# A two-layer gated attention and mixture kernel: results of the first mixture scattered to (choice, token) order, masks counted in the attention, values kept on chip

## The reference, cut to what matters

```python
x = x + tanh(g_xattn[0]) * attn0(layernorm(x), ctx, ctx)          # causal: query i sees keys 0..i
x = x + tanh(g_ffn[0])   * moe0(layernorm(x))                     # 8 experts, 2 choices, silu(a)*b, F = 1024
x = x + tanh(g_xattn[1]) * attn1(layernorm(x), ctx, ctx, mask)    # mask 2048x1601 int32, 0 = not seen
x = x + tanh(g_ffn[1])   * moe1(layernorm(x))                     # 16 experts, 2 choices, capacity 320, shared MLP

# moe0
topk_vals, topk_idx = top_k(xf @ wr.T, 2);  gates = softmax(topk_vals)
for e in range(8):
    a, b = split(xf @ w1[e] + b1[e]);  y_e = (silu(a) * b) @ w2[e] + b2[e]
    out += sum(where(topk_idx == e, gates, 0)) * y_e
```

## Time and profile before

| | us |
|---|---|
| median of 3 runs | 1788.0 (1787.66 to 1790.7) |
| profiled execution, its own time | 1806.31 |
| its span (first to last instruction) | 1804.6 |
| PE busy in the span | 1481.2 |
| DVE busy | 865.0 |
| ACT busy | 669.3 |
| GpSimd busy | 369.1 |
| mean granted TensorE clock | 0.90 of full |

### The profile page before, as it was taken

How to read it: one execution, slowest core, us unless ns; L and a number is a source line. 1 busy time by engine, 2 the same in 40 slices (tenths; PEclk the granted TensorE clock), 3 DMA queues, 4 the chain that set the end, 5 groups by cost and what they waited for, 6 DMA issues and landing times. The chain is left out here.

```text
span 1804.6 us, 25617 instructions
## 1 busy us (share of the span) xinstructions
PE 1481.2 (82%) x8697; PEld 902.9 (50%) x8698; DVE 865.0 (48%) x2072; ACT 669.3 (37%) x1100; POOL 369.1 (20%) x335
## 2 busy tenths in 40 slices
PE   4588999999996454999999994049999766999994
PEld 2343333333335333999999994022333353566662
DVE  4489998888715321222222224439887455211112
ACT  3224556667762011233222221033778421022221
POOL 0000000000020344057705003400000233425531
PEclk9879999999998566999999997577999886999997
DMA  3811203020032349045503201331110031124434
GB/s 108 255 51 43 93 12 112 1 90 3 1 106 95 108 161 233 24 147 195 206 23 111 96 23 44 109 107 35 37 37 2 11 108 39 54 82 140 137 96 155
DMA packets 92052, 157.50 MB, mean 87 GB/s; under 512 B 12102, under 2 KB 71040, under 8 KB 89791
## 3 DMA queue, kind: packets, MB, share of 16 engines
q1 hardware_dynamic: 68959, 77.19, 14.1%
q0 software_dynamic: 19296, 70.86, 11.5%
q10 hardware_dynamic: 3712, 8.39, 1.2%
HBM read 109.29 MB, written 50.12 MB: 88 GB/s over the span
## 5 line engine op out<-in xcount | busy, mean ns | idle before, releaser
L800 DVE TENSOR_REDUCE mxp<-psA 128x1 f32<-128x384 f32 (+4 forms) x640 | 334.7, 577 | 61.2 <-PE psA L656 41.8
L774 ACT ACTIVATE Pt<-psC 128x1024 f32<-128x1024 f32 (+4 forms) x296 | 256.2, 918 | 146.1 <-PE psC L689 74.9
L1353 PE MATMUL psA<-xTt,w 128*128 128x128 f32 x1728 | 203.3, 278 | 4.7 <-issue 4.4
L1353 PEld LDWEIGHTS psA<-xTt,w 128*128 128x128 f32 x1728 | 198.5, 194 | 11.1 <-issue 11.1
L656 PE MATMUL psA<-Kst,Qst 97*128 97x384 bf16 (+4 forms) x640 | 181.6, 350 | 27.1 <-DMA Qst<-q_parts 12.7
L800 DVE TENSOR_REDUCE mxpt<-psA 128x1 f32<-128x449 f32 x256 | 145.2, 619 | 33.9 <-PE psA L656 28.9
L682 PE MATMUL psC<-Qst,Kst 100*128 100x512 bf16 (+4 forms) x592 | 148.9, 355 | 0.7 <-ACT Pt L774 0.2
L1429 DVE SCALAR_TENSOR_TENSOR hT<-psA,b,sil 128x128 f32<-128x128 f32 x216 | 64.2, 345 | 166.3 <-ACT sil L1407 166.3
L774 ACT ACTIVATE Ptt<-psC 128x1024 f32<-128x1024 f32 (+1 forms) x128 | 123.8, 1020 | 47.5 <-PE psC L682 47.1
L656 PEld LDWEIGHTS psA<-Kst,Qst 97*128 97x128 bf16 x640 | 55.3, 99 | 171.2 <-DVE mxp L800 122.6
L705 PE MATMUL psO<-Pt,Vaug 128*17 128x512 f32 (+4 forms) x1184 | 140.8, 546 | 0.0
(11 more groups left out here) (281 smaller groups left out, 2062.8 us busy)
## 6 DMA issues: line engine op xcount, KB each, us to landing
w<-L_w POOLq DMA_DIRECT2D x8, 2048.0 KB
mi<-mask POOLq DMA_DIRECT2D x16, 800.5 KB, 4.9
Kst<-k_parts SPq DMA_DIRECT2D x12, 800.5 KB, 19.1
w<-L_w POOLq DMA_DIRECT2D x8, 1024.0 KB
q_parts<-parts ACTq DMA_DIRECT2D x4, 1536.0 KB, 14.9
Qst<-q_parts SPq DMA_DIRECT2D x48, 128.0 KB, 2.7
Qstt<-q_parts SPq DMA_DIRECT2D x48, 128.0 KB, 2.8
wg<-L_w_gate POOLq DMA_DIRECT2D x16, 352.0 KB
```

Of the source, the lines that this page charges most:

```text
L774: act.activation(Pt[0:kw, n % SLOTS, :, col:QC], psC[0:kw, n % 2, :].rearrange("p (y t) -> p y t", y=2)[:, :, col:QC], ACT.Exp).then_inc(p ...
L800: dve.tensor_reduce(mxp[:, q, h, pc:pc + 1], psA[:, place_of[("piece", n)] % AB, 0:w], AX.X, ALU.max).then_inc(a_free, 1)
L1353: mmi = pe.matmul(bank(j)[:, i * P:(i + 1) * P], w1[:, side, k, f * P:(f + 1) * P], xTt[:, z, k, :], start=(k == 0), stop=(k == KD - 1))
```

## The change

- `Vaug` is one buffer for the whole kernel. The block "c" computes the keys first and the values last, and leaves the values in `Vaug`; their store to DRAM and their reload are gone. Its key parts lie in the room of `Kst`. The block no longer waits until the key parts have landed in DRAM: SP waits for that at the start of `experts0`, then fills the constant rows of `Kst` from a small DRAM copy, and loads the six key parts in three portions behind the weights of experts 3, 4 and 5.
- The weights of the first mixture are loaded by SP, those of experts 0 and 1 in the block of `route`.
- The rows of the first mixture carry labels; GpSimd's scatter runs in four groups of eight, each with an IOTA and a copy ahead of it. In the loop of `experts0` ACT loads rows and labels, DVE multiplies by the gate in a second instruction, and GpSimd scatters the results to `ys` in (choice, token) order. `combine` reads whole chunks on SP and ACT and adds them.
- Mask counting and the bias addition move to GpSimd's program in the attention (the bias in both attentions, the mask in the first).
- The unneeded rows of `ys0` are no longer zeroed.

```diff
+        Vaug = sb(ctx, "Vaug", [P, NKT, H, NV])
-        def load_key_stack(queue, l, Ks, done):
-            for b, (_, kp) in enumerate(PAIRS):
+        def load_key_stack(queue, l, Ks, done, at=0, most=len(PAIRS)):
+            for b in range(at, at + most):
+                kp = PAIRS[b][1]
...
# projections(): the block called "c" keeps its parts in the room of Kst
+                if ql is None:
+                    room = Kst[:, :, :].rearrange("p h s -> p (h s)")
+                    n_parts = NB * 3 * S
+                    parts = room[:, 0:n_parts].rearrange("p (b t s) -> p b t s", b=NB, t=3)
...
+                def stored(eng):
+                    for b in range(NB):
+                        eng.wait_ge(sto[b], 16 * (len(jobs) // NB))
                     @block.sync
...
-                        if ql == 1:
-                            sp.dma_start(Vaug[:, 0:S // P, :, :].rearrange("p j h n -> p j (h n)"),
-                                         Vs[0:S // P].rearrange("j p n -> p j n")).then_inc(vload, 16)
...
+                            sp.dma_start(k_rows_d[0:1, :], zero_row[:, :]).then_inc(rload, 16)
+                            sp.dma_start(k_rows_d[1:4, :], ones_row[:, :]).then_inc(rload, 16)
-                        if kl == 1:
-                            for j, (k0, kw) in enumerate(key_tiles()):
-                                sp.wait_ge(vev, j + 1)
-                                sp.dma_start(Vs[j, 0:kw, :], vout[0:kw, j % VB, :, :].rearrange("p h n -> p (h n)"))\
-                                  .then_inc(v_sto[j % VB], 16)
...
-                        for b in range(NB):
-                            sp.wait_ge(sto[b], 16 * (len(jobs) // NB))
+                        if ql is not None:
+                            stored(sp)
...
                     def _(pe):
-                        if kl == 1:
-                            pe.wait_ge(ld, 48)
-                            values()
...
-                        if kl == 0:
+                        if kl is not None:
                             values()
                     def _(dve):
-                        if kl == 1:
-                            values()
                         for i in range(len(jobs)):
                             split(i)
-                        if kl == 0:
+                        if kl is not None:
                             values()
# attention(): its gpsimd program
                 pool.memset(ones_q[:, :], 1.0).then_inc(ones_made, 1)
+                pool.wait_ge(ones_made, 1)
+                beside(pool)
# output_projection()
-                        sp.dma_start(bob[:, :], w["bo"].rearrange("(a n) -> a n", a=1).to_broadcast([P, D]))\
-                          .then_inc(ld, 16)
-                    @block.gpsimd
...
-                            if c == 1:
-                                dve.wait_ge(bias_s, 1 + NC)
# new, called as beside() in the first attention
+        def count_masks(st):
...
+                pool.memset(ignored[:, :], 0.0).then_inc(counted, 1)
+                pool.wait_ge(counted, 1)
+                load_mask(0)
+                load_mask(1)
+                for t in range(NQT):
+                    pool.wait_ge(mask_ld[t % 2], 16 * (t // 2 + 1))
+                    pool.tensor_scalar(off[:, :], mi[:, t % 2, :], 0, None, ALU.is_equal).then_inc(seen, 1)
+                    pool.wait_ge(seen, t + 1)
+                    pool.tensor_tensor(ignored[:, :], ignored[:, :], off[:, :], ALU.add).then_inc(counted, 1)
+                    pool.wait_ge(counted, t + 2)
+                    if t + 2 < NQT:
+                        load_mask(t + 2)
# attention_layer()
+                def add_bias(pool):
+                    pool.dma_start(bob[:, :], W[L]["bo"].rearrange("(a n) -> a n", a=1).to_broadcast([P, D])).then_inc(bias_ld, 16)
+                    pool.wait_ge(bias_ld, 16)
+                    pool.tensor_scalar(bob[:, :], bob[:, :], gates[:, L:L + 1], 0.0, ALU.mult, ALU.add).then_inc(bias_s, 1)
...
+                        def beside(pool):
+                            add_bias(pool)
+                            count(pool)
# route(): the first mixture's scatter now takes the labelled form too
-                    if width == D:
-                        for t in range(NQT):
-                            for k in range(2):
-                                scatter_tile(pool, t, k)
-                        return
# experts0(), gpsimd program
+                        with pool.Fori(0, pair_count(pool)) as it:
+                            for z in range(2):
+                                pool.wait_ge(ye, it * 2 + (z + 3))
+                                pool.sem_inc(leaving, 1)
+                                pool.indirect_dma_start(
+                                    ys[:, :], bass.IndirectOffsetOnAxis(ap=lab[:, z, 0:1].bitcast(U32), axis=0),
+                                    yv[:, z, :], None, bounds_check=2 * T - 1, oob_is_err=False).then_inc(y_st[z], 16)
+                            for z in range(2):
+                                pool.wait_ge(y_st[z], it * 16 + 16)
+                                pool.sem_inc(yv_free[z], 1)
# experts0(), sync program
-                        for z in range(2):
-                            sp.sem_inc(y_st[z], 16)
-                            load_rows(z * P, z)
-                        load_key_stack(sp, 1, Ks, kload)
-                        with sp.Fori(0, pair_count(sp)) as it:
...
+                        key_parts_stored(sp)
+                        sp.dma_start(Kst[RB:RB + 4, :, :], k_rows_d[:, :].unsqueeze(1).to_broadcast([4, H, SP_])).then_inc(k_rows, 16)
+                        for e in range(2, E0):
+                            last = sp.value_load(ends[0:1, e - 2:e - 1], min_val=2, max_val=NT0 + 2)
+                            sp.wait_ge(w_ld, NW * e)
+                            sp.wait_ge(ye, last)
+                            load_expert(sp, e, w1, w2, w_ld)
+                            if 3 <= e < 3 + len(PAIRS) // 2:
+                                load_key_stack(sp, 1, Ks, kload, 2 * (e - 3), 2)
# experts0(), scalar program
+                        def load_rows(first, z):
+                            act.dma_start(xt[:, z, :], xs[bass.ds(first, P), 0:D]).then_inc(x_ld[z], 16)
...
                             for z in range(2):
                                 x_out(it * 2 + (z + 2), z)
+                                load_rows(it * (2 * P) + (4 + z) * P, z)
+                            for z in range(2):
+                                act.wait_ge(yv_free[z], it + 1)
+                                load_labels(it * (2 * P) + z * P, z)
# experts0(), vector program
-                                dve.wait_ge(y_st[z], it * 16 + 16)
+                                dve.wait_ge(lab_ld[z], it * 16 + 16)
                                 dve.tensor_tensor(yv[:, z, :], bank(4 + z)[:, 0:D],
-                                                  b2[:, bass.ds(experts[z] * D, D)], ALU.add).then_inc(ye, 1)
+                                                  b2[:, bass.ds(experts[z] * D, D)], ALU.add).then_inc(y_sum, 1)
+                                dve.wait_ge(y_sum, it * 2 + (z + 1))
+                                dve.tensor_scalar(yv[:, z, :], yv[:, z, :], lab[:, z, 1:2], None, ALU.mult).then_inc(ye, 1)
# combine()
-                            pool.indirect_dma_start(
-                                yg[:, n % NR, :], None, ys[:, :],
-                                bass.IndirectOffsetOnAxis(ap=slot[:, k, t:t + 1], axis=0),
...
+                        queue.dma_start(yg[:, k, c * QTC:(c + 1) * QTC, :],
+                                        ys[k * T + c * QC:k * T + (c + 1) * QC, :].rearrange("(t p) d -> p t d", p=P))\
+                             .then_inc(y_in[c], 16)
...
+                                dve.tensor_tensor(v, v, yg[:, k, c * QTC:(c + 1) * QTC, :], ALU.add).then_inc(added, 1)
# ffn_layer(), loads(): w1 and w2 of experts 0 and 1 now on SP
+                        load_expert(sp, 0, w1, w2, w_ld)
+                        sp.wait_ge(w_ld, 32)
+                        load_expert(sp, 1, w1, w2, w_ld)
```

More of the change, by code:

```diff
@@ L941, in _, with gpsimd, load_mask @@
                                 mmi.then_inc(mm, 1)
+        def count_masks(st):
+            mi = sb(st, "mi", [P, 2, S], I32)
+            off = sb(st, "mask_off", [P, S], BF16)
+            mask_ld = [sem(f"n_mask_loaded{i}") for i in range(2)]
+            seen, counted = sem("n_mask_seen"), sem("n_mask_counted")
+            def gpsimd(pool):
+                def load_mask(t):
+                    pool.dma_start(mi[:, t % 2, :], mask_d[t * P:(t + 1) * P, :]).then_inc(mask_ld[t % 2], 16)
+                pool.memset(ignored[:, :], 0.0).then_inc(counted, 1)
[10 more added lines that the diff above has]
+                        load_mask(t + 2)
+            return gpsimd
         def summarise_mask(st):
@@ L1268, in experts0 @@
                 yv = sb(st, "yv", [P, 2, D])
```

(18 more changed lines are left out.)

211 lines of the change are left out of this document (75 added, 136 removed).

## The result

The changed kernel takes 1770.85 us (median of 4 runs, 1763.79 to 1773.3) against 1788.28 before: ratio 0.9894, 95% interval 0.9864 to 0.9923. A second set of four runs gave 1769.15 and 0.9879 (0.9856 to 0.9903). By the medians it is faster by 17 to 20 us where 45 were forecast, and 1743 with its range 1718 to 1768 missed it.

What follows compares the result with a forecast made beforehand. PE was taken as near full in the attentions and mixture loop, and waiting in block "c", combine and other gaps. Gains of 66.1 us less losses of 20 and 1 gave -45.1, so 1788.0 became 1743, range 1718 to 1768.

Steps and rivals of the forecast that it cites:

- block "c", -22.1: Keys, values and scatter block: without waits for value stores and key parts' landing it ends 22.1 us earlier, bounds 17 and 24.
- First attention, +21: GpSimd's counting holds DVE's short instructions at four unit ends, 20 us lost (0 to 32), plus 1 for mask traffic.
- rival C: First attention: DVE's 640 maxima are held as well, about 125 us lost, 1848; 4% chance.
- Loop start, -12.2: Start of the first mixture's loop: PE's 12.19 us wait for the second pair's rows goes, lower bound 10.
- The loop: First mixture's loop: added issues, multiplication and scatters lie behind PE's matmuls of the next turn, costed at nothing.
- rival D: First mixture's loop gets longer through a chain of labels, multiplication and scatter: 36 us at 2 a turn, 1779; 5% chance.
- Its end, +3 forecast: Loop's end: second DVE instruction, indirect issue, landing, GpSimd's loop end and register load cost 3 us, between 1.5 and 5.
- Combine, -19.8: Combine: adding whole loaded chunks instead of gathering takes 26.0 us, 22.8 less; net of the loop's end 19.8 (17 to 22).
- Second query projection, -4.2: Second query projection: scaled `bq` no longer arrives behind the reload of the values, saving 4.2 us, bounds 0 and 5.5.
- Output projections, -7.8: Both output projections: DVE's wait for GpSimd's bias and the holding of L878 go, 2.9 and 4.9 us, together 6 to 9.
- Rival A: First attention: nothing is lost, short instructions slip between GpSimd's or PE's queued pieces cover them; 1723, 20% chance.
- Rival B: Upper ends meet: 32 us lost in the first attention and block "c" saves only 17; 1760, 17% chance.

Runs made afterwards that it cites:

- 2nd trace: The kernel before, unchanged, timed and traced again against the kernel before: 1789.09 us, ratio 1.0002, span 1789.0.
- loads only: Changed kernel with the mask's 16 loads but without the two counting instructions per tile, counts set to constants: 1743.87 us, ratio 0.9746.
- key rows late: Changed kernel with the load of the key stack's four constant rows issued behind expert 2's weights: 1758.97 us, ratio 0.9843.
- after: The changed kernel, in its first trace, against the kernel before: 1770.85 us, ratio 0.9894, traced span 1768.4.
- its second trace: The changed kernel, unchanged, timed and traced again: 1769.15 us, ratio 0.9879 against the kernel before.
- counting only: Changed kernel with all 32 counting instructions, but only the first two mask tiles loaded and each counted eight times: 1763.73 us, ratio 0.9862.
- In pieces: Changed kernel with each of the 32 counting instructions beside the attention cut into four of 401 columns: 1747.8 us, ratio 0.9781.

## Why the prediction was wrong, step by step

The step that failed most is **block "c", -22.1**: "PE reaches the keys only at 661.42, because the values wait for their own stores". The rows say so the earlier trace rows, but they are one execution's. Usually the block ends with expert 1's weights, 13.1 us earlier, and what the change saves is 60.0 - 55.5 = 4.5. The prediction had the sign of it in hand: it found the trace 18.3 us above the median and set this aside as 1% of every term. The excess was not spread, it lay in two stretches of 13 and 7 us, and one of them was the largest term. The new end was off as well: 55.5 instead of 51, since 1.3 pass before the first issue, the scatter takes 49.2 instead of 48.6, and 5.05 instead of 2.5 lie between the last issue and the next block. In the ten traces whose block ends with the scatter, with and without key stores that have to land, that last stretch was 4.6 to 5.1; GpSimd's DRAIN of 2.67 in it is the missing part.

**First attention, +21**: the holding was right, the term as a whole too small by 7.7. Four unit ends were held, as forecast, for 5.1 each (5 forecast). The missing term is what PE loses behind the wait, 2.0 us each, 8 in all, by all signs through its clock. "PE waits behind them as long" was too little; it waits, and then works at the lower level for some 8 us. The prediction's own upper bound of 32 had room for it, but for another reason. All kinds of the four instructions were held, L797 and L799 with a single input too. The Trainium skill, "SBUF — State Buffer", section "Who interferes with whom", lets such single-source instructions contend in a 2-port mode, and by that rule the holding would be an estimated 24; measured are 20.4 and 20.9. The prediction took over from it that the later one is blocked for the whole instruction. The traces bear this out for L797 and L799, but not for the two-input L798 and L800 where they met an L929: in all four cases they were through 0.94 to 0.96 before its end. The maxima (L785, PSUM in, 577 ns on average in both kernels) and the reduction L794 (SBUF in and out, 0.22 inside L929 at 135.01 and inside L931 at 221.33, 0.22 before) were not held, so rival C is false.

**Loop start, -12.2**: the 12.19 went (10.76 in the 2nd trace of before). The bound "no key part is under way" overlooked the small load that was in its place: `Kst<-k_rows` cost 7.3 at the first pair's rows. What came of it is -8.8. The kernel before (2nd trace) waits 1.66, 2.10 and 10.76 on PE, 14.5 in all, the changed one 8.52: 6.0 less. The other 2.8 come behind the stall:

```profile
710.91 1.11 PE L1344 MATMUL psC<-ident,xt 128*128 128x128 f32 x4 [10.76 <-DMA xt<-rows]
```

From here PE takes 7.1 us to the first result (717.97) with a granted clock of 0.50 and 0.70, the changed kernel from 727.43 only 4.3 (731.73) at 1.00. Here too the clock was part of the price of a wait, this time on the side of the gain.

**The loop**: right, 375.2 against 375.7; rival D is false. Its end, +3 forecast, is +2.9.

**Combine, -19.8**: -23.0. The block took 24.3 instead of 26.0. Another 1.4 lie behind its last statistic: `wq` was issued 3.0 behind it and is now issued 1.6 behind it, because the two loads of the values no longer stand ahead of it on SP. **Second query projection, -4.2**: -5.6. **Output projections, -7.8**: -3.8 and -6.6. The second attention, expected at nothing, is 1.0 longer; no unit end is held there (L794 0.18, as before), and no run shows whether the bias beside it is the cause. The route's +2.1 goes with PE's granted clock: from 8 to 16 us into the block it was 0.66 and 0.76, where the kernel before had 0.92 and 0.93. The counting does not decide it, for loads only had 40.8 us there and key rows late, with the counting, 38.7; what does is open.

Sum of the differences: 17.6 + 7.7 + 3.4 + 2.1 + 1.0 + 0.3 for the longer, 0.9 + 0.5 + 3.2 + 1.4 + 1.7 for the shorter: 24.4, which is 45.1 - 20.7. Rival A's 1723 fails twice: the holding is there, and without it the kernel runs in 1739.8, 17 above it, since block "c" gives no more there (55.2). Rival B had the attention's side, but its 17 for block "c" was still 12.5 too much, so that 1760 was 11 too low. In rival D the whole gain is gone from 45.1 / 18 = 2.5 us a turn, not from 3.7, and the bounds of the gains, added straight, are 50 and 73, not 52 and 71; neither bears on the miss.

## What to carry to other kernels

When the traced execution is longer than the median, the excess sits somewhere; trace again before a term is built on a long wait that no plain resource explains. Work moved to GpSimd beside a chain of short DVE instructions costs up to the rest of a GpSimd instruction each time they meet, and then some 2 us on top, by all signs through PE's clock: put it where DVE works from PSUM and has slack, or cut it into pieces of a microsecond. Before a stall is booked as gone, look at what small transfers now stand at its place.

## What the runs showed of the hardware

- A short DVE instruction on SBUF alone (0.17 to 0.19 us) took up to 4.42 beside GpSimd's counting. With one input (L797, L799) it ended 0.03 to 0.05 behind the GpSimd instruction that it met, of 3.2 or 4.3 us. With two inputs (L798, L800) it ended so behind an L931 (two inputs, one case), but 0.94 to 0.96 before the end of an L929 (one input, int32 to bf16), in four cases of four. Beside pieces of 401 columns even one-input ones got through (L799, 0.17 inside a GpSimd comparison at 109.99). Where DVE's began 0.01 to 0.02 ahead of GpSimd's it was not held (L798 at 135.67, L931 at 135.68).
- A held unit end costs more than the holding: 2.1, 2.0, 2.0 and 2.0 us more in after, where PE then idled for 4.3 to 6.8 us, 1.6 to 1.9 in its second trace, 1.9 on average in key rows late, 1.6 in counting only. In pieces, with holds of 1.0, 0.1, 1.0 and 0.7, the whole loss is 3.5.
- GpSimd's DRAIN at the end of a block took 2.66 to 2.68 us where the block's last work was the indirect scatter and its landing had been waited for (ten traces), and 0.75 at the end of the first projections.
- With a load of 200 KB for four partitions (68 packets) issued beside them, PE got the first of two loads of 128 KB 9.2 us after the issue, without it 2.2. The DMA views of the two starts, after first and key rows late second, over 8.5 and 8 us; the columns are forty slices of the window, busy tenths of 16 DMA engines:

```profile
DMA  1035992858965455014123141412304313122222
q10 hardware_dynamic: 284, 0.26, 21.9%
q1 hardware_dynamic: 68, 0.21, 17.5%
```

```profile
DMA  0100674788200000006875693000000000000200
q10 hardware_dynamic: 576, 0.52, 23.4%
```

In the first, behind 3.4 us of up to nine tenths, none to four tenths of the engines are busy to the end: few of them still work off the rest of both. That the packets of the rows queue behind the large ones on those few is the likely reading; the engines were not told apart.
- With 3 MB of weights issued by GpSimd behind the scatter, the block of the kernel before ended 12.3 us after the last scatter issue, with them out of it 4.6.
